# Two passes of the input layer norm for the odd tiles: from GpSimd to VectorE

## The reference

```python
x = x + _layernorm(attn(_layernorm(x), Wq, Wk, Wv, Wo))   # causal, rope
x = x + _layernorm(ffn(_layernorm(x), gate_w, up_w, down_w, gate_s, up_s, down_s))
def _layernorm(x, axis=-1, eps=1e-5):
    m = jnp.mean(x, axis=axis, keepdims=True)
    v = jnp.var(x, axis=axis, keepdims=True)
    return (x - m) / jnp.sqrt(v + eps)
```

## Time and profile before

| | us |
|---|---|
| median of 2 runs | 4329.28 (4328.02 to 4330.55) |
| profiled execution | 4323.45 |
| its span, slowest core | 4321.9 (cores: 4293.1 to 4321.9) |
| busy in the span: PE, DVE, ACT, POOL | 3131.0, 1271.4, 739.7, 571.8 |
| first weight load of the second stage, core 7 | 462.26 |

### The profile page before, as it was taken

How to read it: one execution, slowest core, us unless ns; L and a number is a source line. 1 busy time by engine, 2 the same in 40 slices (tenths; PEclk the granted TensorE clock), 3 DMA queues, 4 the chain that set the end, 5 groups by cost and what they waited for, 6 DMA issues and landing times.

```text
span 4321.9 us, 34533 instructions; the slowest of 8 cores (4293.1 to 4321.9 us)
## 1 busy us (share of the span) xinstructions
PE 3131.0 (72%) x12448; PEld 1158.5 (27%) x12448; DVE 1271.4 (29%) x1239; ACT 739.7 (17%) x780; POOL 571.8 (13%) x297
## 2 busy tenths in 40 slices
PE   5544479888889947788888886723888888788870
PEld 1100134333344413111111112200333333333320
DVE  2443325545555538122222220054000000000012
ACT  2211000000000000444444441122000000000000
POOL 0534200000000000233333330000000000000004
PEclk9766689999999979888888888955999999988985
DMA  5463851111111170211111103222333333343323
GB/s 164 128 175 97 143 97 49 54 58 54 54 58 53 40 129 26 62 40 39 40 39 39 40 10 78 39 78 59 59 61 66 59 59 59 63 88 59 54 40 117
DMA packets 183206, 294.32 MB, mean 68 GB/s; under 512 B 6656, under 2 KB 121344, under 8 KB 180864
## 3 DMA queue, kind: packets, MB, share of 16 engines
q0 software_dynamic: 44352, 102.77, 14.3%
q1 hardware_dynamic: 138688, 189.34, 14.0%
HBM read 323.54 MB, written 71.30 MB: 91 GB/s over the span
## 4 chain that ended last, share of the span: by engine, by line
PE 63%; DVE 12%; DMA 7%; POOL 6%; ACT 6%; issue 3%; another core or an unknown queue 2%; POOLq 0%; ACTq 0%; DVEq 0%; SPq 0%
PE psA L159 21%; PE psB L159 19%; PE psD L159 8%; PE psC L159 7%; PE psE L159 6%; POOL lno L271 2%; ACT esb L547 2%; DMA lns<-ln_scr 2%; POOL lno L273 2%; DMA xa<-xctx 2%; POOL esb L557 2%; DVE hdn L737 1%; ACT gt L734 1%; DVE esb L557 1%
## 5 line engine op out<-in xcount | busy, mean ns | idle before, releaser
L159 PE MATMUL psA<-h,gsb 128*128 128x512 bf16 x1408 | 333.2, 398 | 156.9 <-DVE hdn L737 127.2
L557 POOL TENSOR_TENSOR esb<-esb,mask_sb 128x1024 bf16<-128x1024 bf16 x128 | 271.1, 2118 | 804.9 <-ACT esb L547 804.9
L159 PE MATMUL psA<-lns,wk_sb 128*128 128x512 bf16 x1024 | 247.0, 403 | 166.6 <-DMA lns<-ln_scr 90.4
L159 PE MATMUL psB<-h,usb 128*128 128x512 bf16 x1408 | 311.1, 379 | 0.0
L557 DVE TENSOR_TENSOR esb<-esb,mask_sb 128x1024 bf16<-128x1024 bf16 x128 | 104.9, 820 | 568.5 <-ACT esb L547 568.5
L737 DVE SCALAR_TENSOR_TENSOR hdn<-psB,us_sb,gt 128x1024 bf16<-128x1024 f32 x44 | 56.5, 1283 | 721.3 <-ACT gt L734 721.3
L159 PE MATMUL psE<-esb,ones_c 128*1 128x512 bf16 x768 | 243.8, 400 | 0.0
L159 PE MATMUL psD<-wv_sb,lns 128*128 128x512 bf16 x1024 | 234.6, 383 | 11.5 <-DMA wv_sb<-wv 11.5
L159 PE MATMUL psC<-wv_sb,lns 128*128 128x512 bf16 x1024 | 233.2, 381 | 11.4 <-DMA wv_sb<-wv 11.4
L159 PE MATMUL psD<-esb,vsb 128*128 128x512 bf16 x512 | 159.4, 394 | 111.6 <-POOL esb L557 79.1
L159 PEld LDWEIGHTS psA<-h,gsb 128*128 128x128 bf16 x1408 | 139.8, 101 | 351.4 <-issue 208.4
(11 more groups left out here) (156 smaller groups left out, 3210.0 us busy)
## 6 DMA issues: line engine op xcount, KB each, us to landing
xa<-xctx SPq DMA_DIRECT2D x8, 4096.0 KB, 23.9
gsb<-wg POOLq DMA_DIRECT2D x44, 512.0 KB, 5.2
usb<-wu POOLq DMA_DIRECT2D x44, 512.0 KB, 7.3
dsb<-wd POOLq DMA_DIRECT2D x32, 704.0 KB, 6.3
ln_scr<-lno SPq DMA_DIRECT2D x10, 2048.0 KB, 10.5
lns<-ln_scr SPq DMA_DIRECT2D x8, 2048.0 KB, 10.8
k_scr<-kout SPq DMA_DIRECT2D x128, 128.0 KB, 1.8
v_scr<-vout SPq DMA_DIRECT2D x32, 512.0 KB, 2.6
```

What stands on the lines that cost most here:

```text
L159: en.matmul(o, l, r, start=a, stop=z))
L557: en.tensor_mul(b[:], b[:], m)))
```

## The change

For every tile the two passes of `finish(j)` are issued on DVE, and the waits, the semaphore that later waiters look at and the order of the queue follow from the name of the engine. POOL has no work left in the stage. The other queues keep their order.

```diff
-                eng = "v" if j % 2 == 0 else "g"
+                eng = "v"
                 p.wt(eng, sS, cp_tgt[j])
                 srcb = xa[j % 4]
                 if j >= 1:
```

## The result

The changed kernel takes 0.9846 of the time of the kernel before, with an interval of 0.9826 to 0.9867: 1.5% less, or 67 us of 4334 (58 to 75). That is within 2% of no change, though clear of zero. The forecast was 72 us, 1.7%. The ratio leaves out executions in which a die of the chip was disturbed, which the plain medians (4334.11 and 4285.38 us) do not.

The account below looks back on a forecast made before the run. The first stage was taken to be bound by rounds of normalisation, load, sums and broadcasts; its end moves from 462.3 to 390.1 us, so 4329.3 - 72.2 = 4257 us, range 4243 to 4277.

Parts of the forecast that it names:

- the even chain: First stage: normalisation 0, load 3, 2, load 5, 4, load 7, 6, load 9, 8; 262.1 us from normalisation 0 to 8.
- the 30.8 us named beforehand: DVE's own turn per tile, 13.3 + 17.5 us, against 32.8 in the chain; as rival bound 4243 us, chance 0.07.
- the odd one: First stage: chain 1, load 4, 3, load 6, 5, load 8, 7; about 65.5 us for two tiles after the change.
- The sum: End of first stage on core 7: 350.6 + 13.3 + 17.5 + 8.7 = 390.1 us in place of 462.3.
- issue to first sum: Even chain, from SP issuing a load to PE's first sum on it: 97.0 us over four rounds.
- Loads stretch: Rival: denser traffic lengthens each even-chain load by up to 5 us; time 4267 to 4277 us, chance 0.12.
- The covers: First-stage slack ahead of the chain: statistics on DVE 2 to 5 us, the store before normalisation 3 us.
- the 68 us variant: If the long st_b had another cause than POOL and stayed, the gain would be 68 us, not 72.
- one odd row: st_b (1 x 512) on DVE took 10.78 us, ending just behind POOL's pass; its twin took 0.68 us.
- Hidden gain: Rival: only the last normalisation's shortening shows, 15.8 us, time 4313 us; chance 0.03.
- slower: Rival: colliding transfers lengthen chain loads by more than the normalisation saved, from 18 us each on; chance 0.02.
- its own ends (119.2 and 154.0): Forecast ends of normalisations 1 and 2 on DVE; chains were to interleave at 31 to 34 us without touching.

Follow-up runs that it names:

- the two runs that split the change: Against the kernel before: only tile 9 moved to DVE, stage end 447.6 us; only tiles 1, 3, 5, 7 moved, 410.5 us (before 464.4, changed 393.2).
- the run with early loads: Changed kernel with each SP load issued one place earlier, ahead of the store: 0.9771 of the kernel before, stage end 373.6 us against 393.2.
- the second run: The changed kernel once more, as it is: stage end 392.4 us on the mean of the cores, against 393.2 in its first run.
- the run with all on POOL: All ten normalisations on POOL, against the kernel before with only odd tiles there: stage end 506.1 us against 464.4.
- the run with the load ahead of the store: Changed kernel with load j+3 on SP just ahead of the store of tile j, not behind it: stage end 434.6 us against 393.2.
- the fourteen executions of the table: Single executions of the kernel before, the changed kernel (twice) and follow-up variants, read for stage end (322.3 to 506.1 us) and rest of the span.
- statistics first: Changed kernel with statistics of tile j+1 ahead of normalisation j on DVE: stage end 415.4 us against 393.2; with loads also one place earlier, 348.0.
- half stores: Changed kernel with each normalisation and its store in two halves of eight chunks, nothing else: stage end 375.8 us against 393.2.

## Why the prediction was right

The forecast of 4257 us and its mechanism held. By its steps:

- What bounds the stage. That a load waits for a normalisation, with PE's order making the even chain, is shown by the chains before and after, by the two runs that split the change, and by the run with early loads, which took the load off the path and landed on the 30.8 us named beforehand. The forecast was right to add up the even chain, though the odd one was the pace before: four times the 15.8 us saved in the odd chain would have given 63 us up to normalisation 8, where the even chain gives 56 (406.9 less 350.6).
- The passes. 17.5 us on DVE, 8.69 us each, as in the earlier trace rows.
- The sum. 390.1 us forecast for core 7, 396.5 found. The term that was off is "issue to first sum", 97.0 against 102.6 us; the last store, barrier and the wait before them add another 1 us. The forecast took core 7's own loads "for it is the same work on the same core", and that was the weak reason: the length belongs to the pair and the execution. So core 1, which was to gain about as much as core 7, gained 81.8 us (471.97 to 390.17), its loads falling from 27.4 to 23.9 us, and core 7 gained 65.8. The mean over the cores, where this mostly cancels, moved 71.2 us, and in the second run 72.0, against 72.2; which core the forecast was near to is luck. The mean load of the kernel before, 25.6 us, gives 102.4 us for the four loads.
- Loads stretch. The size on core 7 looked like a little of this rival (load 4, in the odd chain, took 27.9 us, over the 27 named as its sign), but not its cause: at the higher density the mean of the eight cores stayed, 25.6 against 25.5 and 25.1 us.
- Statistics, store and port. The covers held where it counts, in the even chain, and they were as thin as forecast. Besides normalisation 1 on three cores (and normalisation 3 on cores 4 and 5 when the kernel ran again), PE on core 1 waited 0.8 to 1.4 us for the st_b of tiles 3, 5 and 7; its other waits for st_b are those of tiles 1 and 9, which both kernels have. The odd normalisations pay that, and the chain does not. st_b took 0.68 us everywhere. POOL's passes were the real cause of the long st_b, as the run with all on POOL shows, so the 68 us variant is out. The forecast read that as one odd row; the trace of before has four of them on each core. How small the cover of the store was, a few us, shows in the run with the load ahead of the store, where it is gone.
- Hidden gain and slower are out: 1.5% less, interval below 1. The forecast held that a change under 2% can hardly be told from none; with an interval 0.4% wide it can. And by its own ends (119.2 and 154.0) the normalisations come up to 35 us apart, not 34, which changes nothing.
- The later stages. The forecast let them last as long as before. Their mean rose by 6.2 us, which would explain the gap between 71 us in the stage and 65 us on the mean span. But over the fourteen executions of the table the rest lies between 3839.1 and 3860.3 us with no order by the length of the first stage, so this is no effect that these runs can show. What makes the rest vary stays open.

The expectations were worse where they touched the queues: I put the sign of statistics first wrong, because I had not asked when the input of the statistics is ready, and I missed the 17 us of half stores, because the store ahead of the load was counted as 0.7 us of issue and not as bytes ahead in the same queue.

## What to carry to other kernels

An engine that is idle 87% of the time can still be on the path with each of its passes in a stage, as POOL was here with all ten: ask which transfer waits for it, and walk the round through each queue, here SP's and PE's. When a large share of the round is a load, look at what the same queue issued just before it. And an order within a queue is good or bad only for one bound: the same swap cost 22 us with late loads and gained 26 us with early ones.

## What the runs showed of the hardware

- A small DVE instruction with two inputs in SBUF waits for the end of a running POOL pass: 1 x 512 elements took up to 17.7 us against 0.68 us, shown as busy, and nine of nine ended 0.54 or 0.55 us behind the pass. One with a single input in PSUM ran inside a pass in 0.68 us.
- Of a load and a store issued 0.6 us apart on SP's queue, the first is served first: 4 MB took 25.0 us behind a 2 MB store and 17.3 us ahead of it; the store 10.6 us ahead of the load and 21.3 us behind it.
- The length of the loads varies by pairs of neighbouring cores and by execution, 23.9 to 27.6 us for the changed kernel.
